# A graph network's edge counts with one code per edge and half-width count matmuls

## The reference

```python
xn = _layernorm(x, axis=-1)
# _rgcn, 8 relations
for r in range(weight.shape[0]):
    mask = (edge_type == r).astype(x.dtype)
    sums = jax.ops.segment_sum(msgs * mask[:, None], dst, num_segments=n)
    cnt = jax.ops.segment_sum(mask, dst, num_segments=n)
    mean = sums / jnp.maximum(cnt, 1.0)[:, None]
    out = out + mean @ weight[r]
z = jnp.concatenate([u, x], axis=1) @ w_gate + b_gate
h = jnp.tanh(u) * z + x * (1.0 - z)
```

## Time and profile before

| | |
|---|---|
| median of 3 runs | 1878.79 us (1878.29 to 1881.19) |
| profiled execution, its own time and span | 1878.8 us, span 1878.8 |
| PE busy | 1794.9 us, 96% |
| DVE busy | 1023.3 us, 54% |
| ACT busy | 478.5 us, 25% |
| POOL busy | 701.1 us, 37% |
| chain that ended last | PE 84%, DVE 6%, ACT 6% |

### The profile page before, as it was taken

The page is one execution under the profiler, slowest core; times in us unless marked ns, Lnnn a source line. Parts: engine busy times, 40 slices in busy tenths (PEclk is TensorE's granted clock), DMA queues, the critical chain, the costliest instruction groups (busy, mean ns, idle before and its releaser), DMA issues.

```text
span 1878.8 us, 28666 instructions
## 1 busy us (share of the span) xinstructions
PE 1794.9 (96%) x9953; PEld 1477.4 (79%) x9953; DVE 1023.3 (54%) x2540; ACT 478.5 (25%) x1055; POOL 701.1 (37%) x609
## 2 busy tenths in 40 slices
PE   6999999999999999999999999954999999999999
PEld 4876689987777778787777887742899888878987
DVE  7888999997254543526354356786632224362311
ACT  3139956662010110101011145243100000111100
POOL 2110000003634435353534444200485552345862
PEclk9999999999999999999999999956999999999999
DMA  4532222224213121231313534110354351113322
GB/s 134 154 109 77 73 86 79 75 67 129 91 38 89 45 72 56 66 86 47 94 33 113 172 84 131 45 46 7 96 164 146 104 156 51 37 55 118 90 73 66
DMA packets 129282, 162.23 MB, mean 86 GB/s; under 512 B 14288, under 2 KB 75368, under 8 KB 128922
## 3 DMA queue, kind: packets, MB, share of 16 engines
q1 hardware_dynamic: 100848, 120.93, 21.5%
q10 hardware_dynamic: 22250, 23.53, 4.0%
q0 software_dynamic: 6080, 16.40, 2.9%
HBM read 135.51 MB, written 25.30 MB: 86 GB/s over the span
## 4 chain that ended last, share of the span: by engine, by line
PE 84%; DVE 6%; ACT 6%; issue 1%; DVEq 1%; DMA 1%; POOL 0%; ACTq 0%; SPq 0%
PE ps L367 22%; PE ps L368 22%; PE ps L369 21%; PE ps L1236 9%; PE ps L892 3%; ACT sc_col L838 2%; ACT sc_row L837 1%; PE ps L1201 1%; DVE w_lo L318 1%; PE ps L881 1%; PE ps L1156 1%; DMA nat<-in_x 1%; ACT w_hi L313 1%; PE ps L1183 1%; PE ps L1211 0%
## 5 line engine op out<-in xcount | busy, mean ns | idle before, releaser
L367 PE MATMUL ps<-w_hi,xt_hi 128*125 128x512 f32 x1320 | 539.0, 408 | 9.1 <-DVE xt_lo L549 3.5
L256 POOL TENSOR_TENSOR w_hi<-w_stage,zero 128x512 fp32r<-128x512 f32 x256 | 276.8, 1081 | 684.4 <-PE ps L369 670.0
L368 PE MATMUL ps<-w_lo,xt_hi 128*125 128x512 f32 x1320 | 523.0, 396 | 0.0
L369 PE MATMUL ps<-w_hi,xt_lo 128*125 128x512 f32 x1320 | 521.5, 395 | 0.0
L259 POOL TENSOR_TENSOR w_lo<-w_stage,w_hi 128x512 fp32r<-128x512 f32 x256 | 346.2, 1352 | 20.1
L367 PEld LDWEIGHTS ps<-w_hi,xt_hi 128*125 128x125 f32 x1320 | 246.6, 187 | 67.1 <-DVE xt_lo L549 4.3
L369 PEld LDWEIGHTS ps<-w_hi,xt_lo 128*125 128x125 f32 x1320 | 246.0, 186 | 63.3
L368 PEld LDWEIGHTS ps<-w_lo,xt_hi 128*125 128x125 f32 x1320 | 246.3, 187 | 53.5
L367 PE MATMUL ps<-xt_hi,w_hi 128*128 128x314 f32 x736 | 250.5, 340 | 1.3 <-DVE ring L2430 0.6
L369 PE MATMUL ps<-xt_hi,w_lo 128*128 128x314 f32 x736 | 225.9, 307 | 0.0
L368 PE MATMUL ps<-xt_lo,w_hi 128*128 128x314 f32 x736 | 225.7, 307 | 0.0
(11 more groups left out here) (392 smaller groups left out, 2390.2 us busy)
## 6 DMA issues: line engine op xcount, KB each, us to landing
w_stage<-in_stream SPq DMA_DIRECT2D x374, 256.0 KB, 2.7
pre<-ring POOLq DMA_DIRECT2D x30, 250.0 KB, 3.8
a_qt<-pre_t SPq DMA_DIRECT2D x18, 312.5 KB, 3.8
a_qt<-pre_t ACTq DMA_DIRECT2D x14, 312.5 KB
pre_t<-ring_t POOLq DMA_DIRECT2D x12, 312.5 KB, 2.8
pre_t<-ring_t ACTq DMA_DIRECT2D x12, 312.5 KB
a_vx<-pre SPq DMA_DIRECT2D x9, 312.5 KB
nat<-pre SPq DMA_DIRECT2D x2, 1250.0 KB
```

The source lines that it names most:

```text
L256: POOL.tensor_tensor(w_hi[:, q, :], w_stage[:, q % NST, :], zero[:].to_broadcast([128, 512]), ALU.add).then_inc(S("hi_done"), 1)
L367: PE.matmul(dst, l_hi, r_hi, start=first, stop=False)
L368: PE.matmul(dst, l_hi, r_lo, start=False, stop=False)
L369: return PE.matmul(dst, l_lo, r_hi, start=False, stop=last)
```

## The change

Each target column is cut in two halves of 314: there are 80 buckets (40 x 2) of single chunks of 128 slots, 240 chunks, instead of 40 buckets of 256-slot groups. An edge's column and row go into one bf16 code (`e_code`), so that the scatter has one scaled one-hot and one matmul. Three bucket numbers share one f32 in the scan (28 rows instead of 40). The count matmul of a chunk is 314 wide and goes to a bank of its own; two chunks are copied by one ACT instruction, and DVE adds each chunk's 314 columns at a start that it loads four at a time. `hot_row` is made for four chunks at once. Groups 0 to 3 are evacuated by ACT without bias, and their biases are added to `nat` and `z` later. DVE zeroes `adj`.

```diff
+SPLIT = 314
+NKEY = 2 * NBUCKET
+FIELDS, NROW = 3, 28
+CHUNK = 128
+NCHUNK = (EDGES + NKEY * (CHUNK - 1)) // CHUNK
-    C_HAND, C_BACK = 32, 86
+    C_HAND, C_BACK = 32, 84
+        def evacuate_plain(g):
+            for m in range(T):
+                wait_bank(ALE, g, m, c0, g0)
+                if g:
+                    ALE.wait_ge(S(f"st{tag}_{m}"), 16 * g)
+                ALE.activation(ring[:, m, :], ps[0:P, m, :], ACT.Copy).then_inc(S("bank_free"), 1)
...
+        DVE.tensor_tensor(key_hot[:], e_row[:].unsqueeze(1).to_broadcast([P, NROW, EW]),
+                          iota16[0:P, 0:NROW].unsqueeze(2).to_broadcast([P, NROW, EW]), ALU.is_equal)
+        split_low_dve(8, 11)
+        DVE.drain()
+        DVE.tensor_tensor(key_weight[:], key_hot[:], e_weight[:].unsqueeze(1).to_broadcast([P, NROW, EW]), ALU.mult)
+        split_low_dve(11, 14)
...
+    def ranks():
+        DVE.tensor_tensor(scan[:], scan[:], key_hot[:], ALU.mult)
...
+        for b in range(NKEY):
+            DVE.tensor_scalar(key_start[:, b, :], e_key16[:], float(b), b_off[:, b:b + 1], ALU.is_equal, ALU.mult)
...
     def scatter_act(c, j):
         ALE.wait_ge(S("sc_hot"), c + 1)
-        if not row_on_dve(j):
-            ALE.activation(sc_row[j][:], sc_lo[j][:], ACT.Copy, scale=e_row1[:, bass.ds(c, 1)])
-        ALE.activation(sc_col[j][:], sc_lo[j][:], ACT.Copy, scale=e_col1[:, bass.ds(c, 1)]).then_inc(S("sc_scaled"), 1)
+        ALE.activation(sc_code[j][:], sc_lo[j][:], ACT.Copy,
+                       scale=e_code[:, bass.ds(c, 1)].bitcast(F32)).then_inc(S("sc_scaled"), 1)
...
+    LEAD_HOT, STARTS = 6, 4
+    def hist_hot(c):
+        if c % 4 == 0:
+            if c >= 8:
+                DVE.wait_ge(S("hi_pe"), c - 4)
+            DVE.tensor_tensor(hot_row[c // 4 % 2][:], iota_by4[:],
+                              slot_row[:, c:c + 4].unsqueeze(1).to_broadcast([128, 128, 4]), ALU.is_equal)
+        if c >= 8:
+            DVE.wait_ge(S("hi_pe"), c - 7)
+        DVE.tensor_scalar(hot_col[c % 8][:], col_key[:], slot_col[:, bass.ds(c, 1)], None,
+                          ALU.is_equal).then_inc(S("hi_dve"), 1)
...
+    def hist_add(c, start):
+        DVE.wait_ge(S("hi_main"), c // 2 + 1)
+        if c:
+            DVE.wait_ge(S("hi_add"), c)
+        o = adj[:, bass.ds(start, SPLIT)]
+        DVE.tensor_tensor(o, o, counts[c // 2 % 4][:, c % 2, :], ALU.add).then_inc(S("hi_add"), 1)
+    def hist_pe(g):
...
+            PE.matmul(ps[0:P, pair_bank(g) + j, 0:SPLIT], hot_row[c // 4 % 2][:, 0:P, c % 4], hot_col[c % 8][:],
+                      start=True, stop=True).then_inc(S("hi_pe"), 1)
...
         for g in range(3):
-            load_bias(g)
-            for c in range((g + 1) * KT, (g + 2) * KT):
+            ahead = (g + 2) * KT - (2 if g == 0 else 1)
+            for c in range((g + 1) * KT, ahead):
                 split_act(c)
+            evacuate_plain(g)
+            for c in range(ahead, (g + 2) * KT):
+                split_act(c)
...
-        mk_zero = sig(ALE.activation(adj[:].bitcast(F32), zero[0:P, :].to_broadcast([P, NBUCKET * NB // 2]), ACT.Copy), "act_step")
+        DVE.memset(adj[:].bitcast(F32), 0.0)
...
+                for c in (2 * (h * per + n), 2 * (h * per + n) + 1):
+                    hist_add(c, starts[c])
+                    if c + LEAD_HOT < NCHUNK:
+                        hist_hot(c + LEAD_HOT)
+                    if c % STARTS == 0 and c + STARTS < NCHUNK:
+                        starts.update(zip(range(c + STARTS, c + 2 * STARTS), hist_starts(c + STARTS)))
...
+        if c == C_GATE - 3:
+            SP.wait_ge(S("gsum"), 1)
+            load_bias_h(2)
...
+    DVE.wait_ge(S("ld_bh"), 32)
+    bias_half(nat, 0)
     for k in range(5, KT):
         feed_dve(k, k)
+        if k == 6:
+            bias_half(nat, 1)
...
     DVE.drain().then_inc(S("rgam"), 1)
+    DVE.wait_ge(S("ld_z"), 32)
+    DVE.wait_ge(S("ld_bh"), 64)
+    for g in range(2):
+        bias_half(z, g)
     for i, w in enumerate((w1, w2)):
         DVE.wait_ge(S("w_round"), i + 1)
```

## The result

| | before | changed kernel |
|---|---|---|
| median | 1878.68 us (1878.29 to 1881.19, 4 runs) | 1862.49 us (1858.72 to 1863.80, 4 runs) |
| ratio, 95% interval | | 0.9905 (0.9893 to 0.9918) |
| profiled execution, span | 1878.8 us | 1860.3 us |

What follows compares the result with a forecast made beforehand. DVE was taken to set the pace in the counts, DVE and ACT together in the scatter, PE before it. From 1878.8 us, +5.5 - 18.2 + 0.7 - 25.3 + 3 = -34.3 gave 1844.5, range 1829 to 1864.

Steps and rivals of the forecast that it cites:

- Step 1: Before the scatter: reworked preparation on DVE, with the zeroing moved there, starts the scatter 5.5 us later (+3 to +9).
- the two prices that the prediction had: Zeroing of adj before the scatter: 10.7 us as on ACT, up to 13.1 at one element a cycle; 12 taken.
- Step 2: Scatter: DVE drops sc_row and waits less for w_hi; 78.3 us instead of 96.5, -18.2 (-15 to -21).
- step 3: Slot decoding and first hots: new small operations, drains and hots replace 2.57 us, +0.7 us.
- Step 4: Count stage, first evacuation to a_hi: DVE work of 145 us plus waits gives 161 against 186.6, -25.3 us.
- the first rival: Wide hot_row in the counts: its operand goes one element a cycle, 0.60 us not 0.33; 1862.6 us in all; 20%.
- the old 10 us of waits: Count stage on DVE: the earlier waits stay, and 29 more register loads add 0.2 us each, 6 us.
- the prediction's own sign: Count stage: forecast wrong if the stage is not near 161 us or PE waits there for anything but DVE.
- every add exposed: Counts: each add waits for the last; at 0.41 us each, 240 adds cost 98 us, 1943 in all; 5%.
- cheaper waits: Counts: loads issued four adds ahead cost nothing, half the other waits go, zeroing takes 10.7; 1830 us in all; 17%.
- Step 5: Late part: bias adds on z delay the clip of w1 and work behind it, where PE already idles; +3 us (0 to +5).
- the rival of the wide hot_row: Counts: hot_row's operand, read in runs of four, goes one element a cycle; 1862.6 us in all; 20%.

## Why the prediction was right, and where it failed

**Step 1, before the scatter: right in its path, 1.4 us short.** DVE reached natural16 at 128.9, where 128.7 was forecast. The miss is the zeroing: 12 us taken, 10.49 measured with 2.72 of issue ahead of it, so 13.2 in all, the upper of the two prices that the prediction had (13.1). TensorE idled 7.93 us, where 4 to 6 were named. That the clock falls behind such a hole was not in the text.

**Step 2, the scatter, and step 3: right.** 77.8 us against 78.3, and 3.3 against 3.3. The prediction's own terms of a scatter step give 4.91 us and not 4.95, so its sum should have been 77.6; the slip is small.

**Step 4, the counts: the term for waits failed.** The work was priced rightly: hot_col 0.21, hot_row 0.33 and not 0.60, which refuses the first rival, and the sum of 145 us. It kept "the old 10 us of waits" (9 in its own reading of the stage) and gave 0.2 to each new load: 16. Measured are 169.85 - 145 = 25. The prediction took the waits of before over, though the old gap between two adds held two pairs of hot instructions and the new one holds one hot_col. With that, each add paid 0.08 us for a wait ahead of its address operation, and about half of the loads 0.10 more. 147 of the 159 adds with only a hot_col before them paid the 0.08, 12 us, and 32 of them the 0.10 as well, 3 us. Most of the 18.4 us that moving the wait took out of the stage is this.

By the prediction's own sign the mechanism was wrong: it is wrong "if the stage from the first evacuation to a_hi is not near 161 us", and the stage took 169.85, with adds 0.52 and not 0.44 apart. The rival "every add exposed" named the mechanism, though at 0.41 an add; the text set it aside by a_hi and a_lo, 0.03 apart on a wait of the same kind. That evidence was of the wrong kind: a_hi and a_lo have no address from a register, so no operation stood behind that wait. The rival "cheaper waits" was right that loads of four can cost nothing, but this holds only with the wait on the add; in the kernel as forecast they cost.

The Trainium skill ("VectorE: DVE Perf Modes", "What auto-detection actually checks") asked only for 16 bits and a step of 1. For hot_row's runs of four the trace now agrees, with 0.33 us for 512 elements, where f32's rate would be 0.60.

**Step 5, late: failed.** It sent the loss through the clip and what is behind it on ScalarE, and took z's landing as the last thing to wait for. Measured are 9.3 us instead of 3. The clip's own delay is not what counts; it was near the forecast, 13.4 us after rgam where 11.1 were forecast. What it left out is that the adds run beside the w_lo that TensorE needs next, and that the new loads stand ahead of weight chunks; the two shares are 4.9 and 4.5 us up to the first late xt_lo. "Where PE already idles" was the false clause: in the changed kernel TensorE stands 5.8 us for w_lo there, and 0 before.

**The numbers.** 1862.5 lies in the range (1829 to 1864) and the sign was right, but the gain is half of the forecast, two of the five steps failed, and the time lies near the edge. That it lies inside is luck in part: the range reached so far because of the rival of the wide hot_row (1862.6), and that rival is refused.

## What to carry to other kernels

In this kernel DVE's queue ran ahead of the engine, and address operations (46 ns) and loads of four addresses (0.34 us) were free as long as it could. A wait put before the address operation took that away, and the count stage lost 18 us by it. Hang such a wait on the instruction that needs it. When work between two dependent instructions is halved, do not carry over the old waits, but look at what the gap covered. And place work that is moved late by which engine it slows beside it and by what its loads stand ahead of: the bias additions of z and their loads cost 9 us in one place and next to nothing in the gaps of the feed.

## What the runs showed of the hardware

- An add on DVE whose wait for the last one stands before its address operation starts 0.20 us after that one's end; with a fixed address it is 0.10. With the wait on the add itself, adds with a hot_col between them are 0.44 apart, as with fixed addresses.
- A register load from SBUF took DVE's queue 0.34 us for four values and 0.60 for eight. It did not show in the engine's time with four values and the wait on the add; with eight, 17 adds came 0.22 us later.
- Zeroing 12,521 words took ScalarE 10.69 us, and DVE 10.49 with 2.72 of issue ahead of it, the same in eight kernels.
- Beside f32 adds of 2,560 elements on DVE and the clips behind them, three GpSimd w_lo took 2.9 us each, without the adds 1.27; the second add took 3.90 us instead of 2.83.
- After TensorE had stood for 7.93 us, its granted clock was 0.50 in the next 6 us; without the hole it was 1.00 there.
